# Three edits to a fused attention and expert kernel: router gates on another engine, projections as three fp32r products, matmuls ahead of a barrier

## The chip, the cores and the metric

The kernel runs on one core of one Trainium2 chip. The metric is the device time of one execution in microseconds (us), taken as the median of several runs. A profiled execution has a span (first to last instruction of the core) and a time of its own, which is a little longer than the span.

## The reference

The input is x, 8 batches of 1024 tokens with 128 features, so 8192 tokens or 64 tiles of 128. Both branches read the normalised x, and the output is x plus both.

```python
xn = layernorm(x)
out = x + attn(xn) + ffn(xn)

# attn: layer norm again, projections, causal linear attention
qkv = xn2 @ qkv_w + qkv_b; gate = sigmoid(xn2 @ gate_w + gate_b)
k = elu(k * gate) + 1; q = elu(q) + 1
out_num = (tril(q @ k.T)) @ v
out_den = sum(q * cumsum(k)) + 1e-6          # out_num / out_den

# ffn: 8 experts, each token uses 2
scores = (xn @ router_w.T + router_b) / temp
# three rounds: rows, then columns (over the tokens of a batch), to sum 1
gates = sinkhorn(scores)
v, idx = top_k(gates, 2); v = v / (sum(v) + 1e-8)
out = sum over both choices of  v * ((relu(xn @ wg[e]) * (xn @ wp[e])) @ wo[e])
```

## The kernel before, in words

The order of every engine's work is written out by hand, and semaphores connect the engines. Names: PE is TensorE, DVE VectorE, ACT ScalarE, Pool GpSimd, SP the queue that issues most DMAs. There are four stages.

**Statistics and logits (to about 45 us).** x arrives in eight loads. DVE makes statistics (`batch_stats`, `block_variances`, `block_scales`, four blocks of 16 tiles). ACT, Pool and DVE write the normalised rows z, PE transposes them into zT, and multiplies by the router and value weights into `lv`.

**Routing beside the first attention groups (about 45 to 94 us).** Attention goes by 16 groups n of four tiles. Routing is one long chain on DVE over 64 tiles x 8 experts: `shift_half`, `spread_maxima`, `shift_columns`, three rounds of `sum_columns`, `column_factors` and `row_factors` (a column sum is a DVE reduction followed by one matmul with ones, `route_sums`), then `first_best`, `second_best`, `members`, `class_bounds`, `gates` and `slots`. The attention steps of groups 0 to 3 stand between these steps in DVE's order. `slots` gives each token its place in the sorted order of experts, and `key(3)` stands behind it.

**The later attention groups (to about 184 us).** A loop n on PE is: `project(n+1, "g")`, the score product of n, `project(n+1, "k")`, the transpose of the keys of n, `project(n+1, "q")`, and four chunks. A chunk is `add_state` (adds to the running state in PSUM, which ACT copies out in `save_state`) and `out_chunk` (masked scores by values, queries by the copied state). A projection is one fp32 matmul with 512 columns, which the profile shows as two instructions. ACT's order in a loop: `tanh_gate(n+1)`, `save_kt(n)` (copies the transposed keys into `ktok`, which `add_state` waits for), `exp_key(n+1)`, `save_state(n,0)`, `relu_key(n+1)`, `save_state(n,1)`, `exp_query(n+1)`, the other states. DVE's order: `finish(n-1)` (divides and adds to the rows), `mask(n)`, `gate_key(n+1)`, `key(n+1)`, `query(n+1)`. In loops 5, 7 and 9 it then does a part of the tables of the experts (`TABLES`). An even loop starts a new half of a batch with four `add_state`, an odd loop has three. Pool meanwhile scatters finished rows to HBM, sorted by the lower expert, one indirect DMA a tile.

**Experts (about 194 us to the end).** When all 64 scatters have landed, SP loads the sorted rows back. 70 tiles go through the lower and 70 through the upper expert of each token. The PE waits from the last `out_chunk` to the first loaded row; this wait is called the barrier here.

The projection of the kernel before is `pe.matmul(psum[:, 0, :], w_in[:, WG], zt, start=True, stop=True)` (and the same for k and q), and the copy of the keys that `add_state` waits for is in `save_kt`.

## Time and profile before

| what | value |
|---|---|
| median of 3 runs | 414.23 us (413.69 to 414.97) |
| the profiled execution, its own time | 412.56 us |
| its span | 410.4 us |
| busy, share of the span | PE 87%, DVE 64%, POOL 63%, ACT 53% |
| mean granted TensorE clock | 0.966 of full speed |

The shares are averages over stages with different limits, so the prediction reads the stages one by one. A fp32 matmul stands in the rows as two instructions, each with its own weight load (PEld). A matmul's duration holds its pipeline latency, so rates are taken from start to start.

### The profile page before, as it was taken

The numbers are of one execution on the slowest core, as the hardware profiler recorded it, in microseconds if no ns is written. First come the engines' busy times: TensorE is split into PE (matmuls) and PEld (weight loads), VectorE is DVE, ScalarE is ACT, GpSimd is POOL, SyncE is SP. The second block draws the span as 40 slices with busy tenths as digits, with TensorE's granted clock in tenths as the row PEclk, the third lists the DMA queues.
The fourth block names the chain that finished last, engine by engine and source line by source line (L and its number), as shares of the span: only waits on it lengthen the run. The fifth ranks groups of instructions, "written<-read, shape, count | busy, mean of one in ns | idle before, by whom it ended". The sixth has DMA issues, their size and how long they took to land.

```text
span 410.4 us, 9656 instructions
## 1 busy us (share of the span) xinstructions
PE 356.5 (87%) x2706; PEld 316.6 (77%) x2706; DVE 262.1 (64%) x805; ACT 218.3 (53%) x479; POOL 257.8 (63%) x340
## 2 busy tenths in 40 slices
PE   0589767788999999981999999999999999999991
PEld 0479435646676766770999999999989999999990
DVE  2999699997577575661466666666556666666651
ACT  1589623333554546441566666666556666666650
POOL 3586999107776556464266666667756666657763
PEclk9999988899999999996899999999999999999996
DMA  6999999802424313225866666655645454544210
GB/s 186 303 340 334 334 306 322 227 3 78 142 97 142 129 64 119 99 97 159 232 178 185 185 179 177 195 167 169 187 115 138 135 142 126 150 125 119 76 46 5
DMA packets 61089, 66.81 MB, mean 163 GB/s; under 512 B 6994, under 2 KB 55902, under 8 KB 61040
## 3 DMA queue, kind: packets, MB, share of 16 engines
q1 hardware_dynamic: 50912, 44.48, 40.4%
q0 software_dynamic: 8672, 21.19, 14.3%
q10 hardware_dynamic: 1456, 0.53, 0.6%
q8 instruction: 25, 0.41, 0.4%
q14 instruction: 24, 0.20, 0.2%
HBM read 26.44 MB, written 40.92 MB: 164 GB/s over the span
## 4 chain that ended last, share of the span: by engine, by line
PE 69%; DVE 17%; issue 4%; DMA 3%; POOL 3%; ACT 1%; SPq 0%; POOLq 0%; DVEq 0%; ACTq 0%
PE psum L1270 28%; PE psum L1281 13%; PE psum L1154 4%; PE psum L1262 4%; PE psum L1219 3%; PE psum L1138 3%; PE psum L1141 3%; POOL out L426 2%; PE psum L1118 2%; PE psum L1057 2%; PE psum L1112 2%; DVE stats L653 2%; PE psum L1126 2%; DMA rows<-in_L_attn_x 2%; PE psum L1233 1%
## 5 line engine op out<-in xcount | busy, mean ns | idle before, releaser
L1270 PE MATMUL psum<-xT,w_now 128*128 128x128 f32 x1120 | 149.3, 277 | 0.0
L1270 PEld LDWEIGHTS psum<-xT,w_now 128*128 128x128 f32 x1120 | 137.6, 194 | 0.0
L998 DVE TENSOR_TENSOR hT<-relu,psum 128x256 f32<-128x256 f32 x140 | 59.0, 421 | 81.7 <-ACT relu L588 81.7
L588 ACT ACTIVATE relu<-psum 128x256 f32<-128x256 f32 x140 | 53.8, 384 | 87.0 <-PE psum L1270 85.6
L407 POOL DMA_INDIRECT by_lower<-rows,slot_u x64 | 63.0, 985 | 53.4 <-issue 34.3
L414 POOL DMA_INDIRECT by_upper<-row x70 | 69.0, 985 | 42.8 <-issue 25.0
L426 POOL DMA_INDIRECT out<-row x70 | 68.8, 983 | 34.4 <-issue 27.6
L581 ACT ACTIVATE w_now<-w_expert 128x512 f32 x140 | 86.7, 622 | 2.5 <-issue 2.0
L1281 PE MATMUL psum<-w_expert,hT 128*128 x560 | 85.5, 276 | 1.2 <-DVE row L1005 1.2
L1281 PEld LDWEIGHTS psum<-w_expert,hT 128*128 128x128 f32 x560 | 73.7, 192 | 1.6 <-issue 1.6
L1005 DVE SCALAR_TENSOR_TENSOR row<-psum,row 128x128 f32<-128x128 f32 x140 | 48.2, 345 | 1.9 <-PE psum L1281 1.9
L1262 PE MATMUL psum<-ident,row 128*128 128x128 f32 x140 | 38.7, 278 | 10.0 <-DMA row<-by_lower 9.3
L991 DVE COPY xT<-psum 128x128 f32<-128x128 f32 x140 | 39.2, 280 | 9.6 <-PE psum L1262 9.5
L1154 PEld LDWEIGHTS psum<-lv,ktok 128*128 128x128 f32 x112 | 17.6, 195 | 21.5 <-ACT ktok L537 11.7
L398 POOL TENSOR_SCALAR rows<-rows,r1p,base_off 128x128 f32<-128x128 f32 x64 | 33.1, 534 | 0.0
L1154 PE MATMUL psum<-lv,ktok 128*128 128x129 f32 x112 | 27.8, 331 | 5.9 <-ACT state L547 2.8
L1262 PEld LDWEIGHTS psum<-ident,row 128*128 128x128 f32 x140 | 20.3, 145 | 10.9 <-DMA row<-by_lower 10.2
L537 ACT ACTIVATE ktok<-psum 128x512 f32<-128x512 f32 x16 | 9.6, 597 | 35.0 <-PE psum L1233 35.0
L1219 PEld LDWEIGHTS psum<-qp,kp 128*128 128x128 f32 x128 | 16.5, 191 | 12.6 <-DVE kp L725 7.1
L1138 PE MATMUL psum<-lv,scores 128*128 128x129 f32 x128 | 25.5, 286 | 0.0
L725 DVE SCALAR_TENSOR_TENSOR kp<-ek,rk 128x512 f32<-128x512 f32 x16 | 11.1, 693 | 19.3 <-ACT rk L531 19.3
L547 ACT ACTIVATE state<-psum 128x129 f32<-128x129 f32 x56 | 15.6, 278 | 13.4 <-PE psum L1154 12.1
(200 smaller groups left out, 461.0 us busy)
## 6 DMA issues: line engine op xcount, KB each, us to landing
by_lower<-blank SPq DMA_DIRECT2D x1, 9100.0 KB, 31.8
row<-by_lower SPq DMA_DIRECT2D x70, 130.0 KB, 3.1
by_upper<-blank SPq DMA_DIRECT2D x1, 9030.0 KB, 61.5
row<-by_upper SPq DMA_DIRECT2D x70, 129.0 KB, 2.1
rows<-in_L_attn_x SPq DMA_DIRECT2D x8, 512.0 KB, 8.3
by_upper<-row POOLq DMA_INDIRECT x70, 3.2
out<-row POOLq DMA_INDIRECT x70, 2.3
w_expert<-in_L_ffn_wg SPq DMA_DIRECT2D x8, 128.0 KB, 2.1
```

What stands on the lines that cost most here:

```text
L407: pool.indirect_dma_start(by_lower, bass.IndirectOffsetOnAxis(ap=slot_u[:, t:t + 1], axis=0), rows[:, t, :], None).then_inc(scattered, 16)
L414: pool.indirect_dma_start(by_upper, bass.IndirectOffsetOnAxis(ap=row[:, q, SLOT_UP:SLOT_UP + 1].bitcast(U32), axis=0), row[:, q, 0:ROW_UP] ...
L426: pool.indirect_dma_start(out_rows, bass.IndirectOffsetOnAxis(ap=row[:, q, TOKEN:TOKEN + 1].bitcast(U32), axis=0), row[:, q, BASE], None, ...
L581: act.activation(w_now[:, n % 3, :], w_expert[:, bass.ds(number, 1), LOW].rearrange("p a f -> p (a f)"), ACT.Copy).then_inc(w_copied, 1)
L588: act.activation(relu[:, n % 2], psum[:, n % 4, 0:FF], ACT.Relu).then_inc(relu_done, 1)
L991: dve.tensor_copy(xT[:, n % 3], psum[:, 6 + n % 2, 0:P]).then_inc(xT_ready, 1)
L998: dve.tensor_tensor(hT[:, n % 3].rearrange("p f t -> p (f t)"), relu[:, n % 2], psum[:, n % 4, FF:2 * FF], ALU.mult).then_inc(h_done, 1)
L1005: dve.scalar_tensor_tensor(target, psum[:, 4 + n % 2, 0:D], row[:, n % NB, by:by + 1], target, ALU.mult, ALU.add).then_inc(y_saved, 1)
L1154: pe.matmul(psum[:, 5, 0:D1], ktok[:, c, :], lv[:, n * G + c, V1], start=(cb == 0), stop=True, skip_group_check=True).then_inc(s_ready, 1)
L1262: pe.transpose(psum[:, 6 + n % 2, 0:P], row[:, n % NB, Z], ident[:]).then_inc(row_turned, 1)
L1270: last = pe.matmul(psum[:, n % 4, at:at + P], w_now[:, n % 3, at:at + P], xT[:, n % 3, :], start=True, stop=True)
L1281: last = pe.matmul(psum[:, 4 + n % 2, 0:D], hT[:, n % 3, f, :], weights, start=(f == 0), stop=(f == FB - 1))
```

## The change

The change has these parts.

- **Statistics.** `block_variances` takes the second root's argument from var directly, which drops a reciprocal and a product; `block_scales` drops a product. One small product (`root2`) is added once, ahead of `shift_half(0)`.
- **Column sums.** `sum_columns` becomes `weigh_rows`, without the reduction. `route_sums` becomes eight matmuls with 64 columns that add in PSUM.
- **Ranks.** `top` writes its comparison to a bf16 tile, and multiplies and reduces there.
- **Gates.** `gates` leaves DVE but for one reciprocal (`invert_gates`, which waits for Pool, ahead of `slots`). 15 products and sums and one scaling go to Pool, between its last base rows and its first scatter.
- **Order.** The attention steps of groups 0 to 2 are laid out anew between the routing steps, on PE, ACT and DVE.
- **Projections.** From group 5 (`SPLIT`) on each of the three projections is three fp32r products: rounded weights by rounded z, the weights' remainder by rounded z, rounded weights by the remainder of z. The weights are divided once (one ACT copy, one DVE difference in loop 3), z once per group (`round_z` on ACT, `divide_z` on DVE).
- **Finish.** From group 3 on `finish` is done in two halves, the first after the second chunk.
- **Barrier.** Behind the last `out_chunk` PE does 36 bf16 products of 448 columns that nothing reads.

```diff
-                link(dve.tensor_reduce(by_b_e(v64[:]), by_batch(rC[:]).rearrange("p b c e -> p b e c"),
-                                       AX_X, ALU.add))
...
             def route_sums(s):
                 pe.wait_ge(route_dve, col_summed(s))
-                pe.matmul(psum[:, ROUTE_BANK, 0:NT], ones[:], v64[:], start=True, stop=True).then_inc(route_pe, 1)
+                target = psum[:, ROUTE_BANK, 0:NT].rearrange("p (b e) -> p b e", e=E)
+                weighted = rC[:].rearrange("p (b c) e -> p b c e", c=C)
+                for c in range(C):
+                    last = pe.matmul(target, ones[:], weighted[:, :, c, :], start=(c == 0), stop=(c == C - 1))
+                last.then_inc(route_pe, 1)
...
+            pool.wait_ge(route_dve, RANKED_STEP)
+            gate(pool.tensor_tensor(rC[:, :, 0:4], rC[:, :, 0:4], rC[:, :, 4:8], ALU.add))
+            gate(pool.tensor_tensor(rC[:, :, 0:2], rC[:, :, 0:2], rC[:, :, 2:4], ALU.add))
...
+            pool.tensor_tensor(gate_scale, gate_scale, top2, ALU.add).then_inc(gates_summed, 1)
...
+            pool.wait_ge(gates_inverted, 1)
...
+            def invert_gates():
+                dve.wait_ge(gates_summed, 1)
+                dve.reciprocal(gate_scale, gate_scale).then_inc(gates_inverted, 1)
...
+            def round_z(n):
+                act.wait_ge(q_ready, n - 1)
+                act.activation(z_high(n), group(n), ACT.Copy).then_inc(z_rounded, 1)
...
+            def divide_z(n):
+                dve.wait_ge(z_rounded, n - SPLIT + 1)
+                dve.tensor_tensor(z_low(n), group(n), z_high(n).bitcast(F32), ALU.subtract).then_inc(z_divided, 1)
...
             def project(n, what):
-                zt = zT[:, n * G:(n + 1) * G, :].rearrange("p g t -> p (g t)")
+                def product(target, w):
+                    if n < SPLIT:
+                        return pe.matmul(target, w_in[:, w], group(n), start=True, stop=True)
+                    pe.matmul(target, w_high[:, w], z_high(n), start=True, stop=False)
+                    pe.matmul(target, w_low[:, w], z_high(n), start=False, stop=False)
+                    return pe.matmul(target, w_high[:, w], z_low(n), start=False, stop=True)
...
             for n in range(EARLY, NG):
-                finish(n - 1)
+                if n == EARLY:
+                    finish(n - 1)
+                else:
+                    finish_half(n - 1, 0)
+                    finish_half(n - 1, 1)
                 mask(n)
+                if n == EARLY:
+                    divide_projections()
                 if n + 1 < NG:
                     gate_key(n + 1)
+                    if SPLIT <= n + 2 < NG:
+                        divide_z(n + 2)
                     key(n + 1)
                     query(n + 1)
...
+            for _ in range(36):
+                pe.matmul(psum[:, 3, 0:K * NT], before_h[:], member[:, 0].rearrange("p k t -> p (k t)"),
+                          start=True, stop=True)
```

Three places in the order of the instructions. First DVE at the end of the routing, from the class bounds of `class_bounds` to the slots; `t`, `u` and `score` are the gate values, `placed` and `slot` the places. Before:

```order
L843 TENSOR_SCALAR class_before<-before_class,class_tilesf 14x14
L714 SCALAR_TENSOR_TENSOR kg<-th,psum 128x512
L847 TENSOR_REDUCE t<-rC 128x64
L848 TENSOR_SCALAR t<-t 128x64
L849 TENSOR_TENSOR u<-score 128x64
...
L862 TENSOR_TENSOR rows<-t,v 128x64
L863 TENSOR_TENSOR rows<-u,score 128x64
L868 TENSOR_TENSOR placed<-psum,member 128x448 x2
L871 TENSOR_REDUCE slot<-placed 128x128
```

Now:

```order
L946 TENSOR_SCALAR class_before<-before_class,class_tilesf 14x14
L819 TENSOR_SCALAR den<-psum 128x4
L822 RECIPROCAL rden<-den 128x4
L827 SCALAR_TENSOR_TENSOR rows<-psum,rden,rows 128x128 x4
L795 SCALAR_TENSOR_TENSOR qp<-eq,psum 128x512
L951 RECIPROCAL score<-score 128x64
L956 TENSOR_TENSOR placed<-psum,member 128x448 x2
L959 TENSOR_REDUCE slot<-placed 128x128
```

The 17 instructions of the gates have gone, one reciprocal has come, and `finish(1)` and `query(3)` now stand ahead of the slots.

Second DVE in the loops 7 and 8, from `query(8)` over the tables of the experts (`rA`, `packed`) to `gate_key(9)` (`kg`). Before:

```order
L720 SCALAR_TENSOR_TENSOR qp<-eq,psum 128x512
L956 MEMSET rA 1x2x2
L957 TENSOR_REDUCE rA<-placed 1x2x70
...
L963 CAST packed_no<-packed 1x18
L736 TENSOR_SCALAR den<-psum 128x4
L739 RECIPROCAL rden<-den 128x4
L744 SCALAR_TENSOR_TENSOR rows<-psum,rden,rows 128x128 x4
L730 TENSOR_TENSOR scores<-psum,causal 128x512
L714 SCALAR_TENSOR_TENSOR kg<-th,psum 128x512
```

Now:

```order
L1052 CAST packed_no<-packed 1x18
L838 TENSOR_SCALAR den<-psum 128x2
L840 RECIPROCAL rden<-den 128x2
L846 SCALAR_TENSOR_TENSOR rows<-psum,rden,rows 128x128 x2
L838 TENSOR_SCALAR den<-psum 128x2
L840 RECIPROCAL rden<-den 128x2
L846 SCALAR_TENSOR_TENSOR rows<-psum,rden,rows 128x128 x2
L813 TENSOR_TENSOR scores<-psum,causal 128x512
L789 SCALAR_TENSOR_TENSOR kg<-th,psum 128x512
L809 TENSOR_TENSOR z_split<-zT,z_split 128x512
```

The finish has become two shorter ones ahead of the mask, and the division of z stands behind `kg`.

Third PE in a late loop, the projections around score and key transpose. Before:

```order
L1112 MATMUL psum<-zT,w_in 128x512
L1219 MATMUL psum<-qp,kp 128x128 x4
L1118 MATMUL psum<-zT,w_in 128x512
L1233 MATMUL psum<-ident,kp 128x128 x4
L1126 MATMUL psum<-zT,w_in 128x512
L1154 MATMUL psum<-lv,ktok 128x129
```

Now:

```order
L1321 MATMUL psum<-qp,kp 128x128 x4
L1208 MATMUL psum<-z_split,w_high 128x512
L1209 MATMUL psum<-z_split,w_low 128x512
L1210 MATMUL psum<-z_split,w_high 128x512
L1329 MATMUL psum<-ident,kp 128x128 x4
L1208 MATMUL psum<-z_split,w_high 128x512
L1209 MATMUL psum<-z_split,w_low 128x512
L1210 MATMUL psum<-z_split,w_high 128x512
L1263 MATMUL psum<-lv,ktok 128x129
```

Each projection is three matmuls at the place where it was one, and nothing else moves.

## Rows read from the trace of the kernel before

**Rows 1.** Windows: stretch, PE, PEld, DVE, ACT, POOL busy us, clock, DMA.

```profile
300.00:360.00 60.00, 60.00 (x540) 60.00 (x540) 35.95 (x124) 37.81 (x84) 39.23 (x41) 1.00 0.47 131
```

**Rows 2.** Timeline of the last block's statistics: start, length, engine, line, tiles.

```profile
34.24 0.25 DVE L665 RECIPROCAL ra<-va 128x16 f32<-128x16 f32 x1
34.52 0.17 DVE L666 TENSOR_TENSOR v<-var,ra 128x16 f32<-128x16 f32 x1
```

**Rows 3.** Timeline of PE: the score product of group 3, behind the routing.

```profile
94.06 1.16 PE L1219 MATMUL psum<-qp,kp 128*128 128x128 f32 x8 [2.66 <-DVE kp L725]
```

**Rows 4.** Timeline of DVE: first of the 17 gate instructions, and the first behind them.

```profile
85.08 0.68 DVE L847 TENSOR_REDUCE t<-rC 128x64 f32<-128x512 f32 x1
...
89.13 1.28 DVE L868 TENSOR_TENSOR placed<-psum,member 128x448 f32<-128x448 f32 x2
```

**Rows 5.** Groups by form, 40 to 190 us: busy us, mean ns, idle before.

```profile
L791 DVE TENSOR_REDUCE v<-rC 128x64 f32<-128x512 f32 x3 | 3.2, 1078 | 0.1
...
L809 DVE TENSOR_TENSOR rA<-rA,rank 128x512 f32<-128x512 f32 x2 | 1.4, 716 | 0.1
...
L853 DVE RECIPROCAL u<-u 128x64 f32<-128x64 f32 x1 | 0.6, 553 | 0.0
```

**Rows 6.** Timeline, a Pool product and a DVE product that meet.

```profile
26.52 1.00 POOL L379 TENSOR_TENSOR w_in<-w_in,w_sum 128x384 f32<-128x384 f32 x1
...
26.79 0.75 DVE L666 TENSOR_TENSOR v<-var,ra 128x16 f32<-128x16 f32 x1
```

**Rows 7.** Groups by form on POOL: a product of 128 columns.

```profile
L360 POOL TENSOR_TENSOR bias_row<-bias_row,w_in 128x128 f32<-128x128 f32 x1 | 0.5, 455 | 0.1
```

**Rows 8.** Timeline of PE: starts of loops 4 and 14, score of 15.

```profile
100.13 1.02 PE L1112 MATMUL psum<-zT,w_in 128*128 128x512 f32 x2
...
171.74 1.02 PE L1112 MATMUL psum<-zT,w_in 128*128 128x512 f32 x2
...
178.98 1.06 PE L1219 MATMUL psum<-qp,kp 128*128 128x128 f32 x8
```

**Rows 9.** Timeline in loop 9, from the query projection to the first state product.

```profile
139.50 1.02 PE L1126 MATMUL psum<-zT,w_in 128*128 128x512 f32 x2
139.70 0.60 ACT L537 ACTIVATE ktok<-psum 128x512 f32<-128x512 f32 x1 [1.59 <-PE psum L1233]
...
140.36 0.48 PE L1154 MATMUL psum<-lv,ktok 128*128 128x129 f32 x2
```

**Rows 10.** Timeline in loop 8, behind a part of the tables.

```profile
128.41 1.02 PE L1112 MATMUL psum<-zT,w_in 128*128 128x512 f32 x2
...
130.37 0.14 DVE L736 TENSOR_SCALAR den<-psum 128x4 f32<-128x4 f32 x1
...
133.65 0.26 ACT L547 ACTIVATE state<-psum 128x129 f32<-128x129 f32 x1
```

**Rows 11.** Timeline of PE: bf16 products of 448 columns and what follows.

```profile
85.36 0.36 PE L1194 MATMUL psum<-class_before,tile_h 14*128 14x448 bf16 x1
85.65 0.36 PE L1189 MATMUL psum<-member,before_h 128*128 128x448 bf16 x1
...
86.25 0.36 PE L1194 MATMUL psum<-class_before,tile_h 14*128 14x448 bf16 x1
86.45 0.17 PE L1197 MATMUL psum<-class_before,ones_h 14*128 14x14 bf16 x1
```

**Rows 12.** Timeline around the barrier.

```profile
180.22 0.96 POOL L407 DMA_INDIRECT by_lower<-rows,slot_u  x1 [2.48 <-DVE rows L744]
...
183.87 0.39 PE L1141 MATMUL psum<-state,qp 128*128 128x129 f32 x2
...
193.59 1.51 PE L1262 MATMUL psum<-ident,row 128*128 128x128 f32 x3 [9.33 <-DMA row<-by_lower]
...
198.42 1.06 PE L1270 MATMUL psum<-xT,w_now 128*128 128x128 f32 x8
```

**Rows 13.** Windows, with the granted clock third from the end.

```profile
187.00:188.00 1.00, 0.00 (x0) 0.00 (x0) 0.00 (x0) 0.38 (x1) 0.69 (x2) 0.92 0.67 233
```

More of the change, by code:

```diff
@@ L78, in sparse_block_kernel @@
             hT = last_use("hT", [P, 3, FB, P])
+        with nc.sbuf_tensor("z_split", [P, NT, P], F32R) as z_split:
+            pass
         zT = sb("zT", [P, NT, P])
@@ L556, in _ @@
             act.activation(rB[:], rA[:], ACT.Exp).then_inc(route_act, 1)
-            for n in range(NG):
+            tanh_gate(1)
+            act.wait_ge(w_step, 6)
+            act.activation(w_high[:, REST], w_in[:, REST], ACT.Copy).then_inc(projections_rounded, 1)
+            exp_key(1)
+            relu_key(1)
+            exp_query(1)
+            save_kt(0)
+            save_state(0, 0)
+            tanh_gate(2)
+            save_state(0, 1)
+            save_state(0, 2)
+            save_state(0, 3)
+            exp_key(2)
+            relu_key(2)
+            save_kt(1)
+            exp_query(2)
+            tanh_gate(3)
+            save_state(1, 0)
+            save_state(1, 1)
+            save_state(1, 2)
+            save_kt(2)
+            save_state(2, 0)
+            save_state(2, 1)
+            save_state(2, 2)
+            exp_key(3)
+            relu_key(3)
+            exp_query(3)
+            save_state(2, 3)
+            for n in range(EARLY, NG):
                 ahead = n + 1 < NG
@@ L823, in members @@
                 step(dve.tensor_tensor(v64[:], rank1, rank2, ALU.max))
+                step(dve.tensor_tensor(is_low, rank1, rank2, ALU.is_gt))
+                assert chain[0] == RANKED_STEP
                 link(dve.tensor_tensor(u64[:], rank1, rank2, ALU.min))
@@ L939, in _ @@
             tile_sums()
+            gate_key(3)
+            class_bounds()
             finish(1)
-            class_bounds()
-            gate_key(3)
-            gates()
+            query(3)
+            invert_gates()
             slots()
-            query(3)
             key(3)
@@ L1117, in project @@
                         pe.wait_ge(qp_done, n)
-                    pe.matmul(psum[:, 1, :], w_in[:, WK], zt, start=True, stop=True).then_inc(k_ready, 1)
+                    product(psum[:, 1, :], WK).then_inc(k_ready, 1)
                 if what == "q":
@@ L1125, in project @@
                         pe.wait_ge(qp_done, n)
-                    pe.matmul(psum[:, bank_q(n), :], w_in[:, WQ], zt, start=True, stop=True).then_inc(q_ready, 1)
+                    product(psum[:, bank_q(n), :], WQ).then_inc(q_ready, 1)
             def out_chunk(n, c):
@@ L1143, in out_chunk @@
                     last.then_inc(o_chunk, 1)
+                elif n >= EARLY and c == 1:
+                    last.then_inc(o_half, 1)
                 elif c == G - 1:
@@ L1198, in route_places, with score @@
                   .then_inc(route_pe, 1)
[L1200 to L1211 removed]
+            def score(n):
                 pe.wait_ge(kp_done, n + 1)
@@ new lines, in _ @@
+            project(0, "k")
+            route_maxima()
+            project(0, "q")
+            route_spread()
+            project(1, "g")
+            project(1, "k")
+            route_sums(0)
+            score(0)
+            project(1, "q")
+            turn_key(0)
+            project(2, "g")
+            add_state(0, 0)
+            route_sums(1)
+            add_state(0, 1)
+            project(2, "k")
+            add_state(0, 2)
+            score(1)
+            out_chunk(0, 0)
+            out_chunk(0, 1)
@@ new lines, in _ @@
+            add_state(0, 3)
+            out_chunk(0, 2)
+            out_chunk(0, 3)
+            route_sums(2)
+            turn_key(1)
+            project(2, "q")
+            project(3, "g")
+            for c in range(G):
+                add_state(1, c)
+                out_chunk(1, c)
+            score(2)
+            turn_key(2)
+            project(3, "k")
+            add_state(2, 0)
+            add_state(2, 1)
+            add_state(2, 2)
+            route_counts()
+            route_totals()
@@ L1247, in _ @@
+            project(3, "q")
+            route_places()
+            add_state(2, 3)
+            for c in range(G):
+                out_chunk(2, c)
+            for n in range(EARLY, NG):
+                ahead = n + 1 < NG
+                if ahead:
+                    project(n + 1, "g")
+                score(n)
+                if ahead:
+                    project(n + 1, "k")
+                turn_key(n)
                 if ahead:
                     project(n + 1, "q")
-                add_state(n, 1)
```

213 lines of the change are left out of this document (110 added, 103 removed).

## The prediction

> **What bounds the kernel now.** I read the windows first, stage by stage. In the expert stage PE is busy all 60 of 60 us [rows 1]; nothing of the change touches it, so what counts is when it starts and with which clock. Then the timeline before it. At the end of the routing PE stood idle 2.66 us for DVE's `kp`, and group 3's score product began at 94.06 us [rows 3]: from the logits to there DVE's chain sets the time. The later attention groups are PE's: the eleven loops 4 to 14 take from 100.13 to 178.98 us, 78.85 us, 7.17 each [rows 8]. Last the barrier: PE's last product starts at 183.87 and the first row is turned at 193.59 [rows 12].
>
> I make the sum in five terms against the profiled execution (412.56 us of its own, span 410.4) and take it off the median, 414.23.
>
> **1. Statistics: 0.5 us saved.** The last block's chain loses a reciprocal and a product, 34.24 to 34.52 and about 0.2 behind it, and one more such product [rows 2]: 0.28 + 0.2 + 0.2 = 0.7. PE has other work in that stretch, so not all comes through. I take 0.5; bounds 0 and 0.7.
>
> **2. Routing: 5.5 us saved.** Step by step on DVE.
> - Gates: from the first of the 17 to the first instruction behind them 85.08 to 89.13, 4.05 us [rows 4]. One reciprocal stays, 0.55 [rows 5]. Saved 3.5.
> - Column sums: three reductions of 1.08 [rows 5], 3.3 with their links.
> - bf16 ranks: two products of 0.72 [rows 5] have bf16 on both sides now. No row shows a DVE product of two bf16 operands. Bounds: nothing, and half of each, 0.7. I take 0.5.
> - One comparison (`is_low`) more: 0.15 lost.
> - The column sums must now come from PE: eight fp32 matmuls, 16 instructions. The score product is 8 instructions of 128 columns, 1.16 us to its last end [rows 3]; twice that, less one latency, is 2.0, and half the columns would make 1.1. In the first round DVE has `key(0)` and `gate_key(1)` beside it, about 1.2 us, and PE first has to finish `project(1, "k")`; I take a wait of 0.85 there. In the second round mask, query and key (1.9) cover it, in the third gate, mask and `finish(0)` (2.8).
> - Pool and DVE get in each other's way. When Pool's product of 384 columns ran 26.52 to 27.52, a DVE product of 16 columns took 0.75 us and ended with it [rows 6]; the same one alone took 0.17 [rows 2]. The first eight of Pool's gate instructions run beside `members`, whose products read SBUF twice. A Pool product of 128 columns takes 0.46 [rows 7] and one of 384 1.00, so the first (256 columns) some 0.73 and those of 64 some 0.3. DVE can wait for the first and for one more: I take 0.8 lost; bounds 0 and 2.
>
> The Trainium skill, "SBUF — State Buffer", section "Who interferes with whom", says that the two engines share a port pair, and that a VectorE product with both inputs in SBUF is fully blocked while a GpSimd operation that reads SBUF holds it. By that rule the edit pays back on DVE at most what lies under Pool's instructions, and the trace agrees (0.75 against 0.17).
>
> The sum is 3.5 + 3.3 + 0.5 - 0.15 - 0.85 - 0.8 = 5.5. Pool is free for its part: its base rows end at about 74 us and the gates' inputs come at about 76; its first eight take 3 to 4 us and are done about 80, while `invert_gates` is reached about 82. If Pool were later, `slots` and `key(3)` behind the reciprocal would wait with it, and PE for `key(3)`. Pool's own scatters start behind the gates, but the gates end about as `slots` does.
>
> **3. Late loops: 1.8 us saved.** A fp32 projection holds PE 0.86 us (139.50 to 140.36 [rows 9]). No row shows a fp32r matmul. Bounds per product of 512 columns: bf16 products of 448 columns follow each other, or what comes next, after 0.20 us (86.25 to 86.45) or 0.29 (85.36 to 85.65) where the operands' partitions differ [rows 11]; the other end is half a fp32 projection, 0.43, one of its two instructions. All dummies and projections have 128 partitions on both sides, so I take the first, scaled to 512 columns: 0.215 to 0.23. Three are 0.65, 0.21 less than now.
>
> The Trainium skill, "FP8 and Floating Point Precision", section "TensorE Precision Notes", says that true FP32 goes in four passes through the array and reduced FP32 reads the four bytes and truncates them. By it a product would be one pass of four, by estimate 0.86 / 4 = 0.215.
>
> Not every 0.21 reaches the end. The query projection hides the copy of the keys: the copy starts 0.20 us behind the key transposes, takes 0.60, and the first state product starts at 140.36, exactly when the projection is through [rows 9]. A shorter projection leaves PE waiting for `ktok` there. So per loop g and k count, 0.43; the chunks behind are a chain through ACT that stays as it is. That holds in eight of the eleven loops, 3.4 us. In loops 6, 8 and 10, behind a part of the tables, DVE sets the time: in loop 8 the finish begins 1.96 us after the loop, and the first state is copied 3.28 after that [rows 10]. There g and k save nothing, and the finish in halves adds one `den` and one reciprocal with their links, 0.4: 1.2 us lost. In loop 3 `divide_projections` (384 columns, about 0.5) stands before `gate_key(4)`: 0.4 lost. 3.4 - 1.2 - 0.4 = 1.8. The rounding of z (0.6 on ACT) stands in the 1.59 us that ACT idles before `ktok` [rows 9]; the difference of z (0.7 on DVE) stands behind `kg`, where DVE waits for ACT's `rk` anyway. Without that cover they would cost up to 1.3 a loop, 14 in all.
>
> **4. End of the attention: 0.5 us saved.** Pool waits for the rows of group 14 (180.22 [rows 12]) and from there scatters eight rows, 1.27 apart, without a wait; group 15's rows are early. The half finish of group 14 can begin when DVE is through with `query(15)`, about 0.5 us before now. Bounds 0 and 0.8.
>
> **5. Clock after the barrier: 1.9 us saved.** The clock fell to half at 187.9 (0.92 in that window [rows 13]), 3.7 us after PE's last work, and the first expert products ran at half clock. The third tile's products start at 198.42 [rows 12]. Three tiles from 193.59 at full rate (rows turned, then 0.89 and 0.11 per tile) would have them at 196.5: 1.9 earlier. The 36 products take 36 x 0.20 = 7.2 us from 184.3, to 191.5; then PE idles 2.1 us, less than the 3.7 after which it fell. Were they 0.29 each they would end at 194.7, 1.1 us too late, and 0.8 would be left of this term.
>
> The sum is 0.5 + 5.5 + 1.8 + 0.5 + 1.9 = 10.2, so 402.4 on the profiled execution's own time and 414.2 - 10.2 = **404.0 us** on the median.
>
> **Rivals.**
> - *The clock falls all the same* in the barrier or just behind it, since little happens on PE around the first rows. For it: it fell after 3.7 us of idleness, and 2.1 is not far off. Then 1.9 is gone: 406.
> - *PE is late for the column sums.* PE's work in the routing is denser, and at half clock each set of sums takes 4 us, not 2. Two or three rounds would each lose 1 to 1.5 us beyond the cover, or Pool's gates would block DVE for 2 us: 4 us gone, 408.
> - *fp32r products overlap badly* (0.29 each, 0.87 a projection): term 3 falls to -1.6, and 407.5 results.
> - *Slower than before: a fp32r product costs 0.43, as one instruction of a fp32 projection.* Then a projection is 1.29 instead of 0.86, and all 33 (g, k and q of eleven groups) lie on PE's path: 33 x 0.43 = 14.2 lost against 0.5 + 5.5 - 1.6 + 0.5 + 1.9 = 6.8 saved: 421.5. It decides from a product of about 0.36 us on. Against it: rows 11 show 16-bit operands at 0.20, and nothing in them tells that four-byte operands in one product would take longer; nothing excludes it either.
> - *DVE becomes the bound of the late loops.* Its work there is 4.4 us a loop, and 0.7 + 0.4 come on top: 5.5 of 6.7. Not likely by itself; with Pool's descriptor work in the way, 409.
>
> **How the numbers follow.** The forecast 0.60, the clock 0.13, late sums 0.10, overlap 0.05, DVE 0.03, fp32r at half rate 0.06, the change without a measurable effect 0.03. The forecast's own range is 401 to 406: no lock and covered sums give 2.5 more, the lower bounds of terms 1, 2 and 4 give 2 less. The range to hold 8 in 10 takes in the clock and the late sums: 400 to 409.5. Within 0.3% is about what a measurement of this kernel can't tell from no change; from the same cases faster by more 0.90, within it 0.03, slower 0.07.
>
> **What would show it.** Group 3's score product should start near 88 us, not 94, with no reduction of `rC` and a wait of under 1 us for the first column sum; small DVE products beside Pool's gates should be stretched. The fp32r matmuls should start 0.21 to 0.23 apart; odd loops should last 6.4 and even ones 6.8, loops 6, 8 and 10 7.8 to 8.5. PE should wait about 0.2 for `ktok` in each loop. The clock should stay at full through the barrier, and the first row should be turned at about 185 us instead of 193.6. Wrong would be: products of fp32r 0.4 apart, a dip of the clock at the first rows, or a `slots` that waits for Pool.

## The result: 4.5 us faster, where 10.2 were forecast

The changed kernel took **409.77 us** (408.98 to 410.83, 4 runs) beside 414.23 for the kernel before (413.69 to 414.97); the ratio is 0.9893, 95% [0.9865, 0.9921]. It is faster, by 1.1%, and 0.27 us outside the range given. Its profiled execution took 410.83 us, span 409.1 (before: 412.56 and 410.4), so the two profiles show 1.3 us of the gain, less than the medians do; the experiments below say which stages vary from one profile to the next.

The timeline of PE in the changed kernel, at the end of the routing:

```profile
77.47 0.49 PE L1263 MATMUL psum<-lv,ktok 128*128 128x129 f32 x2 [0.37 <-ACT state L592]
80.11 0.60 PE L1288 MATMUL psum<-ones_h,member 128*64 128x1 bf16 x14 [2.14 <-DVE member L930]
...
81.69 2.08 PE L1207 MATMUL psum<-zT,w_in 128*128 128x512 f32 x2 [0.55 <-DVE kg L789]
...
90.10 1.89 PE L1207 MATMUL psum<-zT,w_in 128*128 128x512 f32 x2
91.80 1.08 PE L1321 MATMUL psum<-qp,kp 128*128 128x128 f32 x8
```

Group 3's score product starts at 91.80, not at 94.06 [rows 3], and it waits for nothing any more: DVE's `kp` used to be what it waited for. PE itself is late. The same projection that takes 1.02 elsewhere takes 2.08 and 1.89 here. The windows (last three numbers: granted clock, DMA share, GB/s) say why:

```profile
78.00:80.00 2.00, 0.00 (x0) 0.00 (x0) 1.97 (x3) 0.28 (x1) 1.84 (x3) 1.00 1.14 244
80.00:82.00 2.00, 1.08 (x16) 0.91 (x17) 1.86 (x7) 0.33 (x1) 1.75 (x7) 0.90 1.07 305
82.00:91.00 9.00, 9.00 (x39) 5.44 (x39) 7.25 (x19) 1.78 (x4) 2.34 (x9) 0.50 0.15 44
...
132.00:137.00 5.00, 5.00 (x28) 4.60 (x27) 3.10 (x10) 2.25 (x6) 3.35 (x4) 0.66 0.34 124
...
191.00:197.00 6.00, 5.42 (x25) 4.95 (x25) 1.71 (x6) 1.53 (x4) 0.00 (x0) 0.50 0.94 250
```

Three stretches at half clock (1.2 instead of 2.4 GHz): 81.6 to 91.8, 132.8 to 136.2 and 190.8 to 197.7. PE did nothing from 78 to 80 and then worked nine microseconds without a pause at half speed. A fourth lies ahead of them, at 50.9 to 54.3.

A fall of the clock in the routing is not new in itself. The kernel before had three there, 54.7 to 58.1, 61.5 to 65.0 and 75.2 to 78.6. Its windows at the last of them, and where the changed kernel is at half clock:

```profile
76.00:78.00 2.00, 2.00 (x9) 2.00 (x10) 1.90 (x4) 0.81 (x2) 0.00 (x0) 0.50 1.02 311
81.00:91.00 10.00, 8.80 (x69) 5.50 (x67) 9.38 (x34) 3.41 (x9) 0.00 (x0) 1.00 0.11 32
132.00:137.00 5.00, 4.07 (x26) 3.10 (x25) 2.77 (x6) 2.99 (x8) 3.24 (x4) 1.00 0.30 107
```

All of them were over before DVE came to `kp`, for which PE then waited 2.66 [rows 3]; the changed kernel's longest lies on the work just ahead of score(3).

The last stretch is at the first rows. Timeline of PE there, in the changed kernel:

```profile
185.75 3.00 PE L1390 MATMUL psum<-member,before_h 128*128 128x448 bf16 x15
190.78 0.88 PE L1398 MATMUL psum<-ident,row 128*128 128x128 f32 x2 [2.03 <-DMA row<-by_lower]
192.24 0.48 PE L1398 MATMUL psum<-ident,row 128*128 128x128 f32 x1 [0.58 <-DMA row<-by_lower]
192.50 1.92 PE L1406 MATMUL psum<-xT,w_now 128*128 128x128 f32 x8
...
199.87 0.39 PE L1406 MATMUL psum<-xT,w_now 128*128 128x128 f32 x2
```

The first row is turned at 190.78 instead of 193.59 [rows 12], the fifth tile's products start at 199.87: only one tile (1.45) ahead of before.

The late loops, by the starts of score(3) (91.80) and score(15) (176.66); score(8) and score(9) are the other two rows:

```profile
126.19 1.05 PE L1321 MATMUL psum<-qp,kp 128*128 128x128 f32 x8
135.90 1.20 PE L1321 MATMUL psum<-qp,kp 128*128 128x128 f32 x8
...
176.66 1.06 PE L1321 MATMUL psum<-qp,kp 128*128 128x128 f32 x8
```

84.86 us for twelve loops; before, 84.92. From score(8) to score(9) alone it is 9.71.

### The profile page after: what moved, and what is told of

It reads as the page before. It is cut to its first block, busy times and chain, and to the rows that moved or that the text cites. A ratio compares the mean times of both kernels' runs of the same rounds, so it can differ in the third digit from the quotient of the medians.

```text
span 409.1 us, 9939 instructions
## 1 busy us (share of the span) xinstructions
PE 368.9 (90%) x2817; PEld 334.0 (82%) x2817; DVE 263.3 (64%) x813; ACT 224.5 (55%) x491; POOL 266.3 (65%) x356
## 4 chain that ended last, share of the span: by engine, by line
PE 67%; POOL 12%; DVE 9%; issue 4%; DMA 4%; ACTq 2%; ACT 1%; SPq 0%; POOLq 0%; DVEq 0%
PE psum L1406 28%; PE psum L1417 13%; POOL rows L417 6%; PE psum L1263 4%; PE psum L1398 4%; PE psum L1245 2%; POOL out L471 2%; PE psum L1248 2%; PE psum L1321 2%; DMA bias_row<-in_L_attn_gate_b 2%; PE psum L1154 1%; PE psum L1208 1%; PE psum L1210 1%; PE psum L1209 1%; PE psum L1207 1%
## 5 line engine op out<-in xcount | busy, mean ns | idle before, releaser
L452 POOL DMA_INDIRECT by_lower<-rows,slot_u x64 | 65.0, 1016 | 34.5 <-DVE rows L846 16.8
L1248 PE MATMUL psum<-state,qp 128*128 128x129 f32 x112 | 22.9, 288 | 0.0
L1245 PEld LDWEIGHTS psum<-lv,scores 128*128 128x128 f32 x128 | 20.4, 203 | 0.8 <-DVE scores L813 0.7
L1207 PE MATMUL psum<-zT,w_in 128*128 128x512 f32 x30 | 18.6, 725 | 1.7 <-DVE kg L789 1.0
```

Source lines behind the costliest of these rows:

```text
L452: pool.indirect_dma_start(by_lower, bass.IndirectOffsetOnAxis(ap=slot_u[:, t:t + 1], axis=0), rows[:, t, :], None).then_inc(scattered, 16)
L1245: last = pe.matmul(o, scores[:, n % 2, c, :], lv[:, n * G + c, V1], start=True, stop=(cb == 0))
```

## The experiments

I compare stages, since the executions differ by up to 2 us before the routing: `gate_key(0)` started between 46.1 and 48.3 in eighteen profiles whose code is the same up to there. The labels are those of the runs. In the table, "routing" is from score(0) to score(3), "loops" from score(3) to score(15), "to the row" from score(15) to the first turned row, "first tiles" from there to the start of the fifth tile's expert products.

| kernel | routing | loops | to the row | first tiles | median us, ratio to before in its launch |
|---|---|---|---|---|---|
| before | 41.14 | 84.92 | 14.61 | 7.73 | 414.23, 1 |
| changed | 35.56 | 84.86 | 14.12 | 9.09 | 409.77, 0.9893 |
| e1 no products | 35.01 | 84.79 | 14.08 | 8.65 | 408.66, 0.9846 [0.9811, 0.9882] |
| e2 46 products | 35.68 | 84.89 | 14.00 | 6.27 | 405.84, 0.9800 [0.9771, 0.9829] |
| e3 before + 36 products | 40.78 | 84.92 | 14.79 | 7.96 | 413.17, 0.9979 [0.9955, 1.0003] |
| e4 all fp32 | 36.00 | 85.99 | 14.06 | 6.27 | 407.00, 0.9817 [0.9786, 0.9848] |
| m1 46 products, pieces spread | 35.58 | 81.45 | 14.02 | 6.37 | 402.83, 0.9742 [0.9718, 0.9767] |
| m2 the same, waits filled | 32.93 | 81.53 | 14.17 | 6.32 | 400.90, 0.9698 [0.9672, 0.9725] |

The routing column compares the changed kernel with its own variants. Against the kernel before it flatters, since score(0) itself comes 7.95 us after `gate_key(0)` instead of 5.02; from `gate_key(0)` to score(3) it is 43.51 against 46.16.

The stretch at 50.9 is not in that column either. From `gate_key(0)` to score(0) it is 7.1 us in e1, e2 and e4, which had no half clock there, 8.0 in the changed kernel, m1 and m2, which had 3.4 us of it, and 9.9 in k2, which had 10.2.

The other twelve runs (f, h and k) were made where the kernel before itself took 474 to 484 us (medians): loops 4 and 5 together were 12 to 15 us longer, with waits that no other engine of the core ends, the expert stage was longer by 46 and more, and executions of one kernel lay up to 4% apart. Of these "disturbed" runs I use what lies ahead of score(3), and say so where I use more.

### The products in the barrier

```diff
-            for _ in range(36):
+            for _ in range(0 in e1, 46 in e2):
```

e3 puts the changed kernel's 36 behind the attention of the kernel before.

> The changed kernel without the 36 products between attention and the first turned row. Theory of the clock (the products end 2.03 us before the first row, and TensorE's granted clock falls at 190.9 with them as it would without): within 0.5 us of the changed kernel's 409.8, the half-clock stretch over the first rows stays and may begin up to 4 us earlier. Rival (the products do save the 1.9 us that the prediction put on them): 1.9 us slower, about 411.7.

> The changed kernel with 46 products in place of 36: 46 x 0.19 = 8.9 us fill the 8.8 us from the end of attention (181.97) to the first row (190.78). Theory of the clock: the granted clock stays at its full level through the first rows, the expert products there run at 0.64 of a tile's half-clock time, and the end comes 1.4 us earlier (one tile), about 408.4. Rival (the expert stage is paced by DVE and the loads of the rows, not by TensorE): no change, 409.8; the up products of the first four tiles stand 1.92 apart at a full clock too.

> The kernel before with the 36 products added behind its attention, nothing else. They end near 183.9 + 7.0 = 190.9, 2.7 us ahead of its first row at 193.6. Theory of the clock: that gap is longer than the 2.03 us in the changed kernel, in which the clock fell, so it falls here too: 414.2 within 0.7. Rival (the prediction's fifth term): 1.9 us faster, 412.3.

Windows of e1, then of e2, at the same place:

```profile
183.00:186.00 3.00, 0.00 (x0) 0.00 (x0) 0.00 (x0) 0.26 (x1) 1.80 (x2) 0.77 0.37 134
...
190.00:192.00 2.00, 1.74 (x8) 1.74 (x9) 0.30 (x2) 0.00 (x0) 0.00 (x0) 0.50 0.93 228
```

```profile
188.00:190.00 2.00, 1.69 (x12) 1.18 (x11) 0.88 (x3) 0.00 (x0) 0.00 (x0) 1.00 0.95 254
190.00:192.00 2.00, 2.00 (x18) 2.00 (x19) 0.94 (x3) 1.64 (x4) 0.00 (x0) 1.00 0.84 234
```

e1 was expected within 0.5 us of the changed kernel and came out 1.1 below it, 408.66, in another launch. With products up to the first row the clock stays full, and the first tiles take 2.4 to 2.8 us less (6.27 against 8.65 and 9.09); the medians of e1 and e2 differ by 2.8. The 36 products bought nothing in the profiled execution: without them the stage is 0.4 shorter. PE idled 2.03 us behind them and the clock fell at 190.8, exactly when the rows came, and was back at 197.7; in e1 it fell at 184.6 and was back at 194.8. The later fall lies on more of the work: 6.8 us of the first tiles at half clock against 6.0. In e3 the pause was 2.70 and the clock fell at 194.9; the median is not to be told from before, and the 1.9 us of the rival (0.9954) lie just outside the interval. In e4, with the same 36, it was 1.97 and the clock held:

```profile
189.68 0.33 PE L1394 MATMUL psum<-ident,row 128*128 128x128 f32 x1 [1.97 <-DMA row<-by_lower]
190.16 0.33 PE L1394 MATMUL psum<-ident,row 128*128 128x128 f32 x1 [0.16 <-DMA row<-by_lower]
...
191.04 1.06 PE L1402 MATMUL psum<-xT,w_now 128*128 128x128 f32 x8
```

With the same 36 products one kernel thus lost 2.8 us and another did not. The changed kernel itself lost its clock there in all three of its profiles, behind pauses of 2.03, 2.58 (f0) and 3.83 (k1), with first tiles of 9.09, 7.35 and 8.44. That the 0.06 between 1.97 and 2.03 decided is not shown. Over all twenty profiles the first tiles take 5.9 to 6.5 us with no half clock in them, 7.4 to 8.0 with 3.4 us of it (e3, f0), 7.7 with 4.5 (before) and 8.4 to 9.1 with 5.6 to 6.8 (k1, e1, changed).

Of my two theories for e1 the clock's was right (no loss); for e2 its direction was right and its size, 1.4, too small by half; e2's rival, an expert stage paced by DVE and the loads, is out.

### The split of the projections, and the finish in halves

```diff
-        SPLIT = EARLY + 2
+        SPLIT = NG        # e4; the rounding and the differences fall away with it
```

> The changed kernel with the later projections again one fp32 product each (no rounding, no differences, the rest as changed). Theory that the split saves 0.33 us in each undisturbed loop and that the clock's fall in loops 8 and 9 (1.5 us) takes part of it back: 11 x 0.33 = 3.6 less up to 1.5 = 2 to 3.6 us slower, 411.8 to 413.4. Rival (DVE's five busy loops with one more instruction each eat all of it): no change, 409.8, and undisturbed loops of 6.5 in both.

The loops are 1.13 us longer than in the changed kernel, not 2 to 3.6. The whole was expected 2 to 3.6 us slower and came out 2.8 faster, 407.00: in its profile the clock held at the first rows (6.27 against 9.09) and ahead of score(0) (0.85 less), which outweighs the split. Beside e2, of the same launch and at full clock there too, it is 1.16 slower, with loops 1.10 longer: that pair shows what the split is worth as it stood. Loop by loop, from one score product to the next:

| loop | 3 | 4 | 5 | 6 | 7 | 8 | 9 | 10 | 11 | 12 | 13 | 14 |
|---|---|---|---|---|---|---|---|---|---|---|---|---|
| e4, all fp32 with halves | 6.87 | 7.25 | 6.83 | 7.74 | 6.84 | 8.40 | 6.84 | 7.93 | 6.83 | 7.24 | 6.83 | 6.39 |
| changed | 6.70 | 6.92 | 6.50 | 7.75 | 6.52 | 9.71 | 6.66 | 7.94 | 6.52 | 6.92 | 6.50 | 6.22 |
| before | 6.93 | 7.24 | 6.84 | 7.37 | 6.83 | 8.04 | 6.83 | 7.55 | 6.83 | 7.24 | 6.84 | 6.38 |

Two things are to be read there. First, e4 against before: all alike but the three loops behind the tables, which are 0.37 longer each, 1.07 in all. The halves cost that, and in the loops they give nothing; what they give stands behind them, in the column "to the row": 14.61 and 14.79 with the whole finish, 14.00 to 14.17 with halves. Pool's last eight scatters start 0.55 us after score(15) with halves and 1.24 with the whole finish, and up to 0.2 of that is lost again before the row is there. Second, changed against e4: 0.31 to 0.33 saved in a whole undisturbed loop, nothing in loops 6 and 10, and 1.31 lost in loop 8. PE in the changed kernel there:

```profile
130.03 0.49 PE L1245 MATMUL psum<-lv,scores 128*128 128x129 f32 x2 [0.47 <-DVE scores L813]
131.45 0.49 PE L1263 MATMUL psum<-lv,ktok 128*128 128x129 f32 x2 [0.93 <-ACT state L592]
...
132.90 0.64 PE L1248 MATMUL psum<-state,qp 128*128 128x129 f32 x2
```

It waits behind DVE, the clock falls at 132.8, and 0.39 becomes 0.64. In e4 the clock held in this loop.

h3 has 46 products and the whole finish in every loop.

```diff
-                if n == EARLY:
-                    finish(n - 1)
-                else:
-                    finish_half(n - 1, 0)
-                    finish_half(n - 1, 1)
+                finish(n - 1)
```

> 46 products, and the late loops finish a group in one piece again (six DVE instructions instead of eight, no wait for the first half alone). Prediction's fourth term: 0.5 us slower. Rival (loops 6, 8 and 10 are bound by DVE, where two small instructions cost 0.35 to 0.5, and the first half's early start gains nothing elsewhere): 0.5 to 1.5 us faster, and loop 8 under 9.0.

It was one of the disturbed runs (475.30, ratio 0.9824 [0.9763, 0.9885]), so its total says nothing on 0.5 us. Nor does its way to the row, 15.36 beside 15.44 to 15.46 in the other three of its launch: their eight scatters took 12.1 us instead of 9.8. Its loop 6, behind the stall, shows the same 0.37. Timeline of PE in h3, then in the changed kernel, score(6) and score(7):

```profile
122.30 1.05 PE L1317 MATMUL psum<-qp,kp 128*128 128x128 f32 x8
...
129.67 1.05 PE L1317 MATMUL psum<-qp,kp 128*128 128x128 f32 x8
```

```profile
111.92 1.05 PE L1321 MATMUL psum<-qp,kp 128*128 128x128 f32 x8
119.67 1.05 PE L1321 MATMUL psum<-qp,kp 128*128 128x128 f32 x8
```

7.37 against 7.75; four other disturbed runs with halves have 7.74 to 7.76 (f2, f3, h4, k1), while f0, which stalled in loop 5, has 6.92. Of the two theories the rival is nearer for the loops (loop 8 was 7.84, under 9.0). That loop took 7.92, 8.02, 7.85 and 8.42 in f0, f2, h4 and k1, with halves and a clock that held, and 9.68 in f3, where it fell: the 1.3 are the clock's and not the halves'.

### DVE's small operations, spread

```diff
-            TABLES = {5: entries_begun, 7: entry_classes, 9: entry_needs}
+            TABLES = {5: begun_entries, 6: class_lengths, 7: entry_classes, 8: shift_entries,
+                      9: pack_entries, 10: entry_lengths, 11: entry_needs}
```

The same thirteen instructions in the same order, with 46 products at the barrier. Three disturbed runs, and one that was not:

> The changed kernel with 46 products at the barrier, and the three blocks of small operations behind loops 5, 7 and 9 laid out one piece each behind loops 5 to 11. Theory of the clock and of a bound by DVE in three loops: no loop waits long enough for the clock to fall, so loops 8 and 9 (9.1 to 9.2 and 7.3) come to about 7 and the sum from score(3) to score(15) falls from 84.9 to 82 to 83; 2 to 3 us faster than with 46 products alone. Rival (DVE is the bound of every late loop, so the 4.9 us of the pieces are paid wherever they stand): 84.9 again, no gain.

> The kernel with 46 products and the small operations one piece behind each of loops 5 to 11, again, since stalls of 8 to 13 us in loop 4 hid its late loops in the first look. Theory of the clock and of a bound by DVE in three loops: score(3) to score(15) in 82 to 83 instead of 84.9, no half-clock stretch there, 2 to 3 us faster than 46 products alone (0.980 of before), so 0.973 to 0.975. Rival (DVE bounds every late loop): 84.9, ratio 0.980.

> 46 products and the small operations spread over seven loops. Theory (three loops bound by DVE, and the clock falls behind the worst of them): score(3) to score(15) 82 to 83, nothing at half clock there, ratio 0.973 to 0.975. Rival (the same operations cost the same wherever they stand): 84.9, ratio 0.980.

> 46 products and the small operations spread over loops 5 to 11, once more. Theory (three loops bound by DVE, the clock falls behind the worst): where no engine stands still for its instructions, score(3) to score(15) in 82 to 83 us against the 84.9 of the run with 46 products alone, and no half-clock stretch there; ratio 0.973 to 0.976. Rival: 84.9, ratio 0.980.

The three disturbed runs gave 464.70 (0.9826 [0.9755, 0.9897]), 476.04 (0.9875 [0.9821, 0.9928]) and 480.02 (0.9856 [0.9795, 0.9917]): inconclusive. m1 gave 402.83. Its loops take 81.45 instead of 84.89, nothing in them runs at half clock, and loop 8 is 7.47 instead of 9.7:

```profile
124.03 1.05 PE L1330 MATMUL psum<-qp,kp 128*128 128x128 f32 x8
131.50 1.05 PE L1330 MATMUL psum<-qp,kp 128*128 128x128 f32 x8
```

The theory stands, a little better than forecast (82 to 83); the rival, that the pieces cost the same wherever they stand, is out. Measured against neighbours without small operations (6.50 and 6.92 in turn), the pieces still cost 1.4 in loops 6, 8 and 12; the blocks cost 4.8 in loops 6, 8, 9 and 10, of which the clock is 1.3 by e4, and up to 1.9 by the disturbed runs above. The thirteen instructions themselves last 4.9 us (1.29, 2.12 and 1.47 as blocks).

### The routing: filled waits, gates, sums

f2 adds 12 products whose result nobody reads, bf16, 512 columns, to the 46.

```diff
+            keep_busy(9)
             route_counts()
+            keep_busy(1)
             route_totals()
+            keep_busy(2)
             project(3, "q")
```

> The changed kernel with 46 products at the barrier, and 12 idle products of 512 bf16 columns (0.21 us each at the full clock) in the routing's waits: nine ahead of the counts, one ahead of the totals, two ahead of the last query projection. Theory of the clock: the granted clock stays full from 78 to 90, projections, places and attention there take half the time, and score(3) comes 1.5 to 2 us earlier after gate_key(0) (41 instead of 42.8). Rival (DVE's chain of places, slots and kp sets score(3)): less than 0.5 us earlier; if the fillers delay counts or totals, later.

> 46 products, the 12 idle products in the routing's waits, and the spread pieces together. Theory of the clock: score(3) 40.2 after gate_key(0) (43.6 in the changed kernel, seen in two executions before), the late loops as in the run beside it, the end 3 us earlier than there: ratio 0.966 to 0.969. Rival (what the routing gives early is given back later, as the changed kernel gave back its own): no faster than the run beside it.

> The same with 12 idle products in the routing's waits. Theory: score(3) at 40.2 to 41.0 after gate_key(0), loops as beside it, ratio 0.965 to 0.968: 14 us less than before in all, which is what the parts of the prediction came to (10.2) and the filled waits more. Rival (the 3 us won are lost before the end of attention): ratio 0.974.

> The same with the 12 idle products in the routing's waits. Theory: score(0) to score(3) in 33.2 us as in the four executions with them so far (35.6 without), and the end as much earlier: ratio 0.967 to 0.970. Rival (the 2.4 us are lost before the end): 0.974.

Score(0) to score(3) took 33.09, 33.07, 33.34 and 32.93 us in these four, and 35.58 in m1. (The medians of the disturbed three: 463.44, 0.9804 [0.9736, 0.9873]; 477.13, 0.9815 [0.9748, 0.9883]; 475.54, 0.9886 [0.9829, 0.9942].) So the theory of the clock held in all of them, and the rival (DVE's chain alone sets score(3)) is out. From `gate_key(0)` to score(3) it is 40.17, 41.04, 41.37 and 40.98; f2 is the one without the early stretch at half clock. In m2 most of the 2.65 us reach the end: span 398.9 after 401.1 (2.2), median 400.90 after 402.83 (1.9), ratio as forecast. PE of m2:

```profile
76.32 2.11 PE L1343 MATMUL psum<-ones_h,before_h 128*128 128x512 bf16 x9
78.63 0.60 PE L1297 MATMUL psum<-ones_h,member 128*64 128x1 bf16 x14 [0.20 <-DVE member L930]
...
80.21 1.12 PE L1216 MATMUL psum<-zT,w_in 128*128 128x512 f32 x2
...
87.66 1.16 PE L1330 MATMUL psum<-qp,kp 128*128 128x128 f32 x8 [1.79 <-DVE kp L800]
```

The projection takes 1.12 instead of 2.08, and score(3) waits for `kp` again, as in [rows 3]: the routing is DVE's once more. The whole of m2's profile has 0.990 as its mean clock (changed: 0.963); only the early stretch, 49.6 to 53.0, is left at half.

f3 puts the gates on DVE again (17 instructions less the comparison that had moved ahead), h4 the three sums over tiles.

```diff
-            invert_gates()
+            gates()        # f3
```

```diff
                 link(dve.tensor_tensor(rC[:], rB[:], over_e(u64[:]), ALU.mult))
+                link(dve.tensor_reduce(by_b_e(v64[:]), ..., AX_X, ALU.add))        # h4; and one product in route_sums
```

> The changed kernel with 46 products at the barrier and the gates again on DVE between the counts' bounds and the slots; Pool does none of them. By the prediction's second term: score(3) 3.5 us later after gate_key(0) (46.3 instead of 42.8) and as much slower. Rival (the shared port took most of it back: DVE's instructions at 78 to 86 ran 1.05 where 0.31 is usual on Pool and 0.69 where 0.20 is usual on DVE, about 2 us in all): 1.5 us later only.

> 46 products, and the three sums over a batch's tiles again on DVE, with one product each instead of sixteen. Prediction's second term: score(3) 3.3 us later after gate_key(0), less the 0.85 wait for the first sum, so 2.5 later (45.3 instead of 42.8) and as much slower. Rival (DVE waited 0.99 there and 0.47 and 0.94 further on, and a DVE that is later finds less of these waits): 1 us later.

Both are disturbed runs (471.73, 0.9921 [0.9848, 0.9995]; 483.54, 0.9850 [0.9772, 0.9927]), to be read up to score(3). f3's routing takes 36.93, 1.3 longer than with the gates on Pool at half clock (35.6), but 3.8 longer than with them on Pool at full clock (33.1). DVE of f3, from the first gate instruction to the first behind them:

```profile
82.75 0.68 DVE L924 TENSOR_REDUCE t<-rC 128x64 f32<-128x512 f32 x1
...
86.66 1.28 DVE L944 TENSOR_TENSOR placed<-psum,member 128x448 f32<-128x448 f32 x2
```

3.91, and f3's score(3) waits for DVE again:

```profile
91.00 1.16 PE L1309 MATMUL psum<-qp,kp 128*128 128x128 f32 x8 [2.68 <-DVE kp L774]
```

So the gates' move made DVE's own path as much shorter as forecast, and in the changed kernel PE's path at half clock became the longer one and hid two thirds of it. By its size f3's rival (1.5 later) is nearer, but the shared port, its reason, is 0.8 only. A run with the gates on DVE and the clock held was not made. h4 takes 37.35. Its score(2) waits 2.30 for `kp` and comes 19.60 after score(0) (changed: 17.24), so two of the three sums cost 2.4 of DVE's path; at score(3) it waits for nothing and 1.8 is left, between its theory (2.5) and its rival (1).

f3 shows the port too. DVE of f3, and Pool and DVE of the changed kernel:

```profile
75.95 0.20 DVE L902 TENSOR_SCALAR cls<-v 128x64 f32<-128x64 f32 x1
...
76.28 1.09 DVE L904 TENSOR_TENSOR member<-cls,class_no 128x896 bf16<-128x896 f32 x1
```

```profile
77.91 0.72 POOL L429 TENSOR_TENSOR rC<-rC 128x256 f32<-128x256 f32 x1 [3.64 <-DVE score L925]
77.99 0.69 DVE L928 TENSOR_SCALAR cls<-v 128x64 f32<-128x64 f32 x1
...
78.82 1.24 DVE L930 TENSOR_TENSOR member<-cls,class_no 128x896 bf16<-128x896 f32 x1
79.19 1.05 POOL L431 TENSOR_TENSOR score<-score 128x64 f32<-128x64 f32 x1
```

`cls` takes 0.69 instead of 0.20 and ends with Pool's addition; `member` takes 1.24 instead of 1.09, and Pool's small addition beside it 1.05 where its neighbours take 0.32. With `class_before` (0.40 against 0.22) DVE loses 0.82. The Trainium skill, "SBUF — State Buffer", section "Who interferes with whom", says that a `tensor_scalar` can claim the shared ports although it has only one input in SBUF, and that whoever issues first blocks the other for its whole length; both directions are in these rows.

### The changed kernel again, and m2 without the split

> The changed kernel once more, beside the three that follow. In its profile the clock fell 2.03 us after the 36 products ended, and in a kernel with the same products but a pause of 1.8 us it did not: its own executions should spread over about 2.5 us, 407 to 410, as the clock holds at that place in some of them and not in others. Rival (the spread comes from the loads at the start): the profile's attention end moves with the start of gate_key(0), and the first expert tile follows it by a constant 17.9 us.

> The changed kernel beside the three that follow. Theory of the clock: score(3) 43.5 after gate_key(0), 84.9 on to score(15), and from the end of attention to the steady expert stage 17.9 us where the clock falls behind the products and about 15.4 where it holds; ratio 0.989 where it falls, down to 0.983 where it holds.

> The kernel with 46 products, idle products and spread pieces, but all projections one fp32 product. Theory of the split's worth: undisturbed loops of 6.83 instead of 6.50 (fewer DVE instructions, longer products), 12 loops: 3 to 4 us slower than with the split, ratio 0.974 to 0.978. Rival (the split gains only as much as the clock and DVE give back): within 1 us of the run with the split.

All three are disturbed: 467.15 (0.9882 [0.9802, 0.9961]), 485.61 (1.0004 [0.9950, 1.0058]) and 481.53 (0.9892 [0.9837, 0.9948]); what was expected of their ends was not tested, and in k1 the changed kernel was no faster than the kernel before. The routing of the changed kernel took 35.59 in f0, and only 34.18 in k1, where the half-clock stretch lasted from 78.8 to 82.2 and score(3) waited 1.53 for `kp`. The same program thus varies by 1.4 there with the length of the stretch (k2, whose order is the same up to there, took 36.52, with an early stretch that reached past score(0)). In k4 the routing took 33.28 like in the others with filled waits. Whether the split is still worth its 0.32 a loop once the pieces are spread stays open; e4 against e2 and against the changed kernel are the only clean pairs, both with the blocks.

## Why the prediction was wrong, step by step

What stood for the clock was one term and one rival at the barrier, and part of a rival at the column sums. The clock fell in three places that the forecast took to be at full clock, and holding it there gives 2.65, 1.3 and 2.8 us, more than the missing 5.7. The sign that the prediction had named for being wrong, a dip of the clock at the first rows, came.

1. **Statistics (0.5): not seen.** `gate_key(0)` started at 48.29, before at 47.90. Starts of it scatter over 2.2 us with identical code, so a gain of 0.5 can't be told.
2. **Routing (5.5): 2.65 on the profiles, from `gate_key(0)` to score(3) (46.16 to 43.51).** The failed step is that DVE's chain would still set the end: nothing in the working asked what PE's granted clock would be once PE had less reason to work between the sums and the counts. The prices themselves were good: gates 3.91 with the reciprocal of 0.54 that stays, so 3.4 (3.5 forecast), two column sums 2.4 (2.2), port 0.82 (0.8), first column sum waited for 0.99 (0.85), of the ranks 0.72 became 0.42 to 0.55 (0.5 for two; one of the comparisons that feed them took longer). With the waits filled, m2 has 40.98 from `gate_key(0)`: 5.2 us less than before, beside 5.5.
3. **Late loops (1.8): 0.06.** The failed step is "per loop g and k count, 0.43": three products take 0.78 from start to start, 0.26 each and not 0.215 to 0.23, which saves 0.08 and not 0.21. A loop still gives 0.31 to 0.33, because the fp32 instruction ahead of a fp32r product makes way about 0.08 sooner as well: at group 5's k projection the last score instruction starts at 99.27 and the product at 99.31, where the distance is else 0.11. The wait for `ktok` behind the query projection was there as forecast: 0.93 from its first product to the first state product (100.44 to 101.37), 0.15 more than the three products take (a wait of 0.2 was forecast). All loops together gave 2.46 where 3.4 - 0.4 = 3.0 were booked. The loss behind the tables was right, 1.07 for 1.2. Not in the working was that PE, waiting there, loses its clock: 1.31 in loop 8. 2.46 - 1.07 - 1.31 = 0.08.
4. **Halves, at the end (0.5): 0.49** (14.61 to 14.12). Right, and by the way forecast: Pool's last eight scatters start 0.69 earlier behind score(15). Together with term 3 the halves are a loss of 0.6.
5. **Barrier (1.9): -1.36** (7.73 to 9.09). "2.1 us, less than the 3.7 after which it fell" was the failed step. One fall behind 3.7 us of nothing does not show that 2.1 are safe; it fell behind 2.03, 2.58 and 3.83 in the changed kernel and held behind 1.97 in e4. Products up to the row give 1.46 against before (6.27), so the mechanism was right, its size somewhat less, and the number of products wrong.

Between the two profiles: 0.39 lost, 2.65, 0.06 and 0.49 gained, 1.36 lost, 0.11 lost in the steady expert stage: the 1.3 by which the spans differ. The medians differ by 4.5, since the kernel before's profile was faster than each of its timed executions (412.56; 413.69 and up) and the changed kernel's was the slowest of its four. Which stages made those four differ is not shown; the stretch ahead of score(0) (0.85 us between an execution with 3.4 us of it and one with none), the routing (34.2 to 35.6 in its three profiles) and the first tiles (7.4 to 9.1) are the candidates.

The rival that PE would be late had the right engine and the half clock, but the wrong place: two of the three column sums were not waited for, the projections and places at half clock were.

A slip in the range: "no lock and covered sums give 2.5 more" is 0.8 + 0.85 = 1.65 by the terms themselves. It moves the low end of the forecast's own range to about 402.4 and leaves the range to hold 8 in 10 as it is.

## What to carry to other kernels

When work leaves the engine that sets the pace, look at each stretch in which TensorE now waits, and at what it does just behind it: a pause of 2 us was followed by ten microseconds at half clock here, nine of them full of work, and twelve products that nobody reads won 2.65 us. Filler must reach to the next real work; filler that ended 2.0 us ahead of it only moved the fall onto that work. And of 4.9 us of small instructions on a second engine the loops paid 3.5 where they stood in three blocks (without the clock), and 1.4 in seven pieces in its waits: the pieces were worth 3.4 us (at least 1.3 of it the clock), more than the split of 33 projections (2.5). m2, with 46 products, spread pieces and filled waits, is the fastest version measured, 400.90 us, 0.9698 of before.

## What the hardware showed that I had not expected

- A fp32r product of 512 columns holds TensorE 0.24 to 0.31 us: 98.26 to 98.50 at the end of three, 0.31 from the first to the second (97.72 to 98.03). The rows' mean durations (488 and 402 ns) hold the pipeline latency and the loops at half clock too. Groups by form, the whole attention:

```profile
L1208 PE MATMUL psum<-z_split,w_high 128*128 128x512 f32 x33 | 16.1, 488 | 0.0
...
L1210 PE MATMUL psum<-z_split,w_high 128*128 128x512 f32 x33 | 13.3, 402 | 0.0
```

- The length of a half-clock stretch isn't fixed: 81.6 to 91.8 in the changed kernel, 78.8 to 82.2 in another execution of the same code (k1).
- A product of two bf16 operands takes DVE 0.42 to 0.55 us for 512 columns, where fp32 took 0.72 [rows 5]; with a fp32 input and a bf16 output it took 0.69 to 0.77, nothing saved.
